# A second staging tile for x, and the batch sort moved into the first projections of a fused attention, MLP and adapter kernel

## What is computed

```python
q, k, v = x @ Wq, x @ Wk, x @ Wv
attn_out = softmax(q @ k.T * 512**-0.5) @ v @ Wp + bp          # per batch
cms_out = gelu(attn_out @ cW1 + cb1) @ cW2 + cb2 + one_hot(target)[:, None, :]
modifier = gelu(concat([attn_out, cms_out]) @ mW1 + mb1) @ mW2 + mb2
z = clip(x + cms_out + modifier, 0, 1)

h = gelu(z @ W_down[role] + b_down[role])                      # 512 -> 256
y = z + h @ W_up[role] + b_up[role]
out = layer_norm(y) * gamma[role] + beta[role]
```

## Time and profile before

| | |
|---|---|
| median of 3 runs | 2073.11 us (2072.64 to 2078.01) |
| profiled execution | 2075.36 us |
| its span, first to last instruction | 2073.8 us |
| mean granted TensorE clock | 0.996 |
| busy share: PE, DVE, ACT, POOL | 97%, 67%, 46%, 5% |
| chain that ended last, share of PE | 85% |

### The profile page before, as it was taken

The page is one execution under the profiler, slowest core; times in us unless marked ns, Lnnn a source line. Parts: engine busy times, 40 slices in busy tenths (PEclk is TensorE's granted clock), DMA queues, the critical chain, the costliest instruction groups (busy, mean ns, idle before and its releaser), DMA issues.

```text
span 2073.8 us, 28655 instructions
## 1 busy us (share of the span) xinstructions
PE 2020.6 (97%) x9396; PEld 1677.2 (81%) x9397; DVE 1398.5 (67%) x2597; ACT 955.2 (46%) x1977; POOL 99.1 (5%) x184
## 2 busy tenths in 40 slices
PE   7999999999999999999999999999999999999997
PEld 6878888888878888888878888888878888887876
DVE  5676786555777686555777686555677685555886
ACT  4654444433654454333654444333654444334554
POOL 0000000000000000000000000000000000000222
PEclk9999999999999999999999999999999999999999
DMA  4011233215111143215111143215111132114544
GB/s 163 28 52 53 65 129 107 90 49 202 63 51 61 58 136 107 84 54 203 62 51 61 51 142 107 76 62 203 62 52 61 51 122 61 49 44 144 176 123 106
DMA packets 111934, 187.86 MB, mean 91 GB/s; under 512 B 12285, under 2 KB 72192, under 8 KB 107456
## 3 DMA queue, kind: packets, MB, share of 16 engines
q1 hardware_dynamic: 98672, 126.19, 19.4%
q0 software_dynamic: 13136, 60.04, 8.4%
HBM read 145.82 MB, written 40.37 MB: 90 GB/s over the span
## 4 chain that ended last, share of the span: by engine, by line
PE 85%; DVE 7%; SPq 3%; issue 2%; ACT 2%; DMA 1%; ACTq 0%; POOL 0%; DVEq 0%; POOLq 0%
PE y L1675 15%; PE y L1677 15%; PE y L1676 15%; PE x L1675 13%; PE x L1677 12%; PE x L1676 12%; SPq L450 1%; DVE w_lo L1103 1%; PE y L1756 1%; DVE f L1227 1%; PE x L1781 1%; SPq L451 1%; DVE a_forms L1272 1%; DMA w_blocks<-w1c 1%; SPq L459 1%
## 5 line engine op out<-in xcount | busy, mean ns | idle before, releaser
L672 ACT CAST w_hi<-w_blocks 128x512 fp32r<-128x512 f32 (+1 forms) x464 | 231.6, 518 | 131.1 <-PE y L1677 83.6
L1103 DVE TENSOR_TENSOR w_lo<-w_blocks,w_hi 128x512 fp32r<-128x512 f32 (+1 forms) x464 | 249.6, 564 | 56.2 <-ACT w_hi L672 56.2
L1675 PE MATMUL x<-h_hi,w_hi 128*128 128x512 f32 x512 | 199.6, 390 | 3.1 <-ACT f L725 3.1
L1675 PE MATMUL y<-h_hi,w_hi 128*128 128x512 f32 x512 | 199.7, 390 | 1.9 <-ACT p_copy L725 1.9
L1677 PE MATMUL x<-h_hi,w_lo 128*128 128x512 f32 x512 | 199.3, 389 | 0.0
L1677 PE MATMUL y<-h_hi,w_lo 128*128 128x512 f32 x512 | 199.2, 389 | 0.0
L1676 PE MATMUL x<-h_lo,w_hi 128*128 128x512 f32 x512 | 199.2, 389 | 0.0
L1676 PE MATMUL y<-h_lo,w_hi 128*128 128x512 f32 x512 | 199.2, 389 | 0.0
L1675 PE MATMUL y<-a_forms,w_hi 128*128 128x512 f32 x480 | 188.1, 392 | 2.1 <-DVE f L1206 1.2
L1677 PE MATMUL y<-a_forms,w_lo 128*128 128x512 f32 x480 | 186.8, 389 | 0.0
L1676 PE MATMUL y<-a_forms,w_hi 128*128 128x512 f32 x480 | 186.8, 389 | 0.0
(11 more groups left out here) (231 smaller groups left out, 4259.9 us busy)
## 6 DMA issues: line engine op xcount, KB each, us to landing
w_blocks<-w1m SPq DMA_DIRECT2D x128, 256.0 KB, 4.2
w_blocks<-w1c SPq DMA_DIRECT2D x64, 256.0 KB, 3.2
w_st<-w2c SPq DMA_DIRECT2D x64, 256.0 KB, 3.3
w_st<-w2m SPq DMA_DIRECT2D x64, 256.0 KB, 4.7
x_hi_lo<-x_halves POOLq DMA_DIRECT2D x6, 2048.0 KB, 11.2
zs<-z_by_batch SPq DMA_DIRECT2D x68, 128.0 KB, 2.1
cms<-f SPq DMA_DIRECT2D x32, 256.0 KB, 2.7
z_cms<-cms POOLq DMA_DIRECT2D x8, 1024.0 KB, 6.4
```

Of the source, the lines that this page charges most:

```text
L672: nc.scalar.copy(w1_hi[:, w % RING, cols], src).then_inc(w1_hi_s, 1)
L1103: nc.vector.tensor_tensor(w1_lo[:, w % RING, cols], src, f32(w1_hi[:, w % RING, cols]), ALU.subtract).then_inc(w1_lo_s, 1)
L1675: nc.tensor.matmul(ps, w[0], x[0], start=first, stop=False, skip_group_check=more)
```

## The change

- A second staging tile `x_st2`, placed in the memory that `v_hi_lo` uses later. SP loads the second tile's x into it at the start, behind the first tile's x and ahead of the role vector; POOL's load is gone, with its wait.
- ACT casts the second tile's x after query 0 and not after query 1. DVE makes its four low parts in one row, after query 1.
- `sort_gather` on PE comes after query 2 and not after scores(1), and writes bank Y[2] in place of X[3]. `sort_pairs` on DVE comes after query 3 and not after v_lo of block 0.
- On DVE `split_a(0, 4)`, `split_a(0, 5)` and `onehot_bias` move from ahead of attention(0) to behind `row_max(0)`, and so ahead of the first `inverse`.

```diff
         with ExitStack() as at_cf:
             x1 = sb("x1_hi_lo", [P, 2, DC, TOK], F32R, at_cf)
             t1 = sb("t1_hi_lo", [P, 2, DC, TOK], F32R, at_cf)
+            with ExitStack() as at_v:
+                x_st2 = sb("x_st2", [P, DC, TOK], on=at_v)
             v_hl = sb("v_hi_lo", [P, 2, 2, D], F32R, at_cf)
             x2 = sb("x2_hi_lo", [P, 2, DC, TOK], F32R, at_cf)
         c_form = sb("c_forms", [P, NF, 2, TOK], F32R)
-        forms = (a_form, c_form)
+        forms, x_sts = (a_form, c_form), (x_st, x_st2)
...
-        sort_bank = X[3]
+        sort_bank, slots_bank = X[3], Y[2]
...
             sp.dma_start(x_st[:], xT[0]).then_inc(x0_loaded, 16)
+            sp.dma_start(x_st2[:], xT[1]).then_inc(x_loaded, 16)
             sp.dma_start(role_i[:], role).then_inc(sort_in, 16)
...
-            pool.wait_ge(x0_loaded, 16)
-            pool.wait_ge(x_lo_s, DC)
-            pool.dma_start(x_st[:], xT[1]).then_inc(x_loaded, 16)
             for s in range(NS):
...
                 for c in range(DC):
-                    nc.scalar.copy(xs[t % 2][:, 0, c, :], x_st[:, c, :]).then_inc(x_hi_s, 1)
+                    nc.scalar.copy(xs[t][:, 0, c, :], x_sts[t][:, c, :]).then_inc(x_hi_s, 1)
...
                     query(s, c)
-                    if s == 0 and c == 1:
+                    if s == 0 and c == 0:
                         split_x(1)
...
-                link(nc.vector.tensor_copy(slots[:].rearrange("o v n k -> o (v n k)"), sort_bank[0:1, 64:64 + 3 * NSLOT]))
+                link(nc.vector.tensor_copy(slots[:].rearrange("o v n k -> o (v n k)"), slots_bank[0:1, 64:64 + 3 * NSLOT]))
...
-                nc.vector.tensor_tensor(x[:, 1, c, :], x_st[:, c, :], f32(x[:, 0, c, :]),
+                nc.vector.tensor_tensor(x[:, 1, c, :], x_sts[t][:, c, :], f32(x[:, 0, c, :]),
                                         ALU.subtract).then_inc(x_lo_s, 1)
...
                 for c in range(DC):
                     query(s, c)
-                    if s == 0 and c:
-                        split_x(1, c - 1)
                     if s:
                         z1_clip(s - 1, c)
+                    if s == 0 and c == 1:
+                        for i in range(DC):
+                            split_x(1, i)
                 if s == 0:
-                    split_x(1, DC - 1)
+                    sort_pairs()
                 query(s, DC)
                 row_max(m0)
+                if s == 0:
+                    for i in (4, 5):
+                        split_a(0, i)
+                    onehot_bias()
...
                 split_v(m0)
-                if s == 0:
-                    sort_pairs()
...
-            for i in (4, 5):
-                split_a(0, i)
-            onehot_bias()
             for s in range(NS):
                 attention(s)
...
                 for v in range(3):
-                    ins = nc.tensor.matmul(sort_bank[0:1, 64 + v * NSLOT:64 + (v + 1) * NSLOT], batch_f[:, v:v + 1],
+                    ins = nc.tensor.matmul(slots_bank[0:1, 64 + v * NSLOT:64 + (v + 1) * NSLOT], batch_f[:, v:v + 1],
...
                 for c in range(DC):
                     query(s, c)
+                    if s == 0 and c == 2:
+                        sort_gather()
                 query(s, DC)
                 scores(m0)
                 query(s, DC + 1)
                 scores(m0 + 1)
-                if s == 0:
-                    sort_gather()
```

## The result

| | before | changed |
|---|---|---|
| median (7 runs each) | 2073.11 us | 2067.34 us |
| lowest to highest | 2072.18 to 2078.01 | 2066.17 to 2069.37 |
| profiled span | 2073.8 us | 2066.9 us |
| mean granted clock | 0.996 | 0.997 |

The ratio is 0.997, with a 95% interval of 0.996 to 0.998: 5.8 us faster, inside the 0.3% that the forecast took as its bound for no change, but clear of zero. The forecast was 2067.2.

What follows compares the result with a forecast made beforehand. PE was taken to bound the kernel. Terms 1.33 + 2.85 + 1.42 + 1.59 - 1.23 - 0.08 = 5.88 us took the median from 2073.11 to 2067.2, range 2063.9 to 2071.8.

Steps and rivals of the forecast that it cites:

- What bounds the kernel: PE, busy 2020.6 of 2073.8 us; only its standstills or low clock can give time, four losses in attention(0)'s first pass.
- The load: SP's load of x_st2 delays the role vector's landing to near 22.0; 0.3 us of cover left, delay costed at 0.
- Query 2: On PE in attention(0): starts at 38.35, 1.33 us earlier, with a wait of 0.42 left.
- Query 4 and the low clock behind it: On PE: starts at 44.61; its 2.85 us wait and the 1.42 lost at low clock both go.
- The new wait before project_v(0): PE waits 1.23 us for weight block 7's low part on DVE, plus 0.08 of slower restart; bounds 0 to 2.2.
- The wait before output(0): PE's wait of 1.59 us there goes; output(0) starts at 64.21.
- The sum: Gains at query 2, query 4 and output(0), less the new wait and its restart: 5.88 us.
- The median: Whole kernel: goes from 2073.11 to 2067.2 us, 5.9 less, or 0.28%.
- The rival of a fallen clock: The clock falls once in the new wait before project_v(0): 1.42 us lost, 2068.7; chance 0.10.
- The slower rival: Clock falls at the new wait, stays down through attention's first steps; 20 us would lose 9.4, giving 2076.6; chance 0.03.
- no clock term: At the new wait before project_v(0), nothing was charged for a low clock; a low stretch's like is 1.42 us.

Runs made afterwards that it cites:

- d1: The changed kernel with one more MB loaded between x_st2 and the role vector; 2069.32 us, ratio 0.9977.
- a1: The kernel before with only the second staging tile and SP's load added, all work in its old order; 2073.39 us, ratio 0.9999.
- a2: The changed kernel with one staging tile and POOL's load as before, so only the order is new; 2067.15 us, ratio 0.9968.
- a3: The kernel before with only the split of the second x reordered on ACT and DVE; 2069.33 us, ratio 0.9979.
- c1: The changed kernel with DVE's one-hot bias moved behind t_lo of query 7; 2066.66 us, ratio 0.9958.
- b2: The changed kernel with the gather and the pair sort back in their old places and bank; 2069.72 us, ratio 0.9975.
- e1: The changed kernel itself, run again in a later session; 2068.10 us, ratio 0.9960.
- d2: The changed kernel with DVE's four one-hot instructions issued twice more ahead of the low part of weight block 7; 2070.41 us, ratio 0.9981.
- b1: The changed kernel with DVE's two weight splits and the one-hot bias back ahead of attention(0); 2068.80 us, ratio 0.9973.
- a4: The kernel before with only the gather and the pair sort moved; 2072.55 us, ratio 0.9991.
- c2: c1 with ACT's splits of weight blocks 4 and 5 also moved behind t_hi of query 0; 2066.43 us, ratio 0.9959.
- c3: c2 with one staging tile and POOL's load as in the kernel before; 2065.77 us, ratio 0.9948.

## Why the prediction was right

- **What bounds the kernel**: right. PE's four losses in 38 to 70 us were the whole matter; the lead was still there at the adapter (5.9 by R, 6.2 there, where the scatter is up to 3 us).
- **The load**: right. The shift of 2.3 (19.5 to 21.8) stayed inside the cover; d1 showed what lies beyond it. That the load itself brings nothing followed from POOL's own load landing 5 us ahead of its use, and a1 and a2 show it.
- **Query 2**: right in its start (38.35 against 38.14). The wait left there was put at 0.42 and measured 1.64, since PE itself came 1.4 earlier in this execution. The start is set by ACT and DVE, so the sum was not touched.
- **Query 4 and the low clock behind it**: right, 2.85 + 1.42. a3 gives them alone: 4.45 in the median, and 4.3 in the profile once the 1.6 of its own low stretch is taken off.
- **The new wait before project_v(0)**: right in place, cause and size (1.23 against 1.09). c1 removes it by moving one step of the chain. I had not seen how much of it hangs on the gather; b2 showed that (0.53 of the 0.69 by which t_lo(4) moves).
- **The wait before output(0)**: right; it is gone, and back in b2.
- **The sum**: 5.88 against R's 5.89. That it fits to 0.01 is luck: errors of 0.05 to 0.14 cancelled. The new wait came 0.14 shorter, while query 7 ended 5.54 earlier and not 5.59 (counted from the role vector), and project_v(0) and (1) took 5.73 and not 5.66.
- **The median**: it moved by 5.77 and came within 0.14 us of the forecast, which is luck too. In other sessions the change was 8.25 under the kernel before (e1, 0.9960) and its equal 6.63 (a2, 0.9968), with the change's R as it was, so the ratios fell just beyond 0.3%, on the faster side. Where those further 0.7 to 2.4 us come from is not shown.
- **The rival of a fallen clock**: it did not come in either profile of the change. But its argument was weak. I had read from three waits that only the longest is followed by the low clock. a3 fell behind 1.84 us of idle time, d2 did not behind 2.79. b1 waited 1.90 idle at the same place as a3 and kept its clock. The length of a wait does not by itself decide it. That the new wait got no clock term came out right in both profiles, but not for the reason given.
- **The slower rival**: no run shows a low clock long enough; a4's, the longest seen in this stretch, cost about 1.5 more than the earlier trace rows (R of 47.72 against 46.2).

## What to carry to other kernels

When PE stands still for a split or a cast, look first at what the engine that makes it does ahead of it, before blaming the load: here the order of the instructions was worth all of the gain, and the staging tile nothing. Write down the chain for the new order instruction by instruction from the old rows; it finds the wait that will open as well as those that close, and the idle place on the same engine where its longest passenger can go (c1). Judge a change of a few us by a distance inside the trace between two rows that it spans; it repeated to 0.05 us for the changed kernel, where medians scattered by 1 to 3. A low clock inside the stretch is part of it (1.6 us in a3), so look at the granted clock there before comparing two of them.

## What was not expected of the hardware

- Where PE's clock falls differs between executions of like kernels. It fell behind 1.84 us of idle time in a3, not behind 2.79 in d2, and stayed low past 54 us in a4 where it had recovered by 51 in the earlier trace rows.
- One fall is in every profile: PE idles 4.9 us ahead of the adapter's first bias row, waiting for DVE, and the granted clock falls to its 1.2 GHz level in that wait or behind it. By the trace it stayed there for 3.4 us in four of the fourteen profiles (that of the kernel before and the first of the changed kernel among them) and for 6.8 in ten. The change does not touch this.
- PE's start-up at the low clock ended at about 13.3 us in one profile and 10.2 in the next with the same work ahead of it, and at 10.0 to 13.3 over all fourteen; the 1.4 us so gained vanished in the next wait for DVE. The Trainium skill ("TensorE: Matmul & The Clock Gate", "What's actually happening") says that the point at which the clock rises varies between runs by about half a microsecond. The runs agree that it varies; the size, 3.1 us between two profiles, does not agree. A kernel that has removed the wait (c2, c3) passes on part of the luck: c2's PE was 0.64 ahead of c3's at the gather, and 0.2 of it was left in R, since t_lo(1) and t_lo(2) on DVE held c2 up.
- The same 1 MB load by POOL took 5.4 us in the earlier trace rows and in a4, 5.6 in a3, 6.0 in a2 and 8.1 in c3.
